# Attention and FFN block in float32: interleaved projections, or projections first by seven block products

## The chip, the core and the metric

The kernel runs on one core of a Trainium2 chip. The core has a matrix engine (TensorE, in the profile PE, its weight loads PEld), a vector engine (VectorE, DVE), a scalar engine (ScalarE, ACT), a general engine (GpSimd, POOL) and a queue engine (SyncE, SP). Each works off its own list of instructions in order and waits on semaphores for the others. SyncE, GpSimd and ScalarE can issue DMAs between DRAM and the on-chip memory SBUF. TensorE writes only to PSUM, eight banks of 128 partitions by 512 float32. The metric is the device time in microseconds, a median of three runs.

## The reference

The input x is 4 batches of 512 tokens by 1024, all float32.

```python
xn = _layernorm(x, axis=-1)
# attention: 32 query heads, 8 key/value heads, head size 128
qkv = xn @ w_qkv                      # 1024 -> 4096 + 1024 + 1024
scores = einsum('bqhgd,bkhd->bhgqk', q, k) * scale
bias = where(rel >= 0, -slopes * sqrt(rel), -inf)      # causal, per head
attn = softmax(scores + bias, axis=-1)
attn_out = einsum('bhgqk,bkhd->bqhgd', attn, v).reshape(B, S, 4096) @ w_o
# FFN: one 1024 x 1024 linear layer, and a routed low-rank part
ffn = xn @ W.T + b
probs = softmax(xn @ gate_w.T + gate_b)                # 4 ranks: 8, 16, 32, 64
ffn += weight * (xn @ A[:r].T @ B[:, :r].T)            # r of the top choice
return x + attn_out + ffn
```

## The kernel before

Float32 products are made from three passes. Every operand is split into a high part (float32r, written by ScalarE, `high`, L572) and a low part (the rest, subtracted by VectorE, `low`, L735), and `product` (L306 to L308) multiplies high by high, high by low and low by high into the same PSUM bank. A "product" of two tiles is thus three matmuls.

The work is cut into two pairs of batches (1024 tokens, eight tiles of 128). For each pair the tokens are loaded into `acc`, which is also the accumulator of the whole result. They are normalised by ScalarE (L645), transposed by TensorE (L360) and split into `x_hi` and `x_lo`, tile by tile (`before_groups`). Meanwhile TensorE already multiplies the tile before with the FFN weights. Then come the gate, the masks of the low-rank part, and the keys, values and first query of group 0. The transposed x stays in SBUF for the whole pair.

Then loops run over eight groups (one key/value head with four query heads), and in each over eight units (a query head and a batch). One unit is: causal scores of four row tiles (`scores`), maxima with the bias on VectorE (L766), exponentials on ScalarE (L605), a division by the row sum on VectorE (L777), ten transposes of 128 by 128 (L438), their split (L572, L735), and attention times values (`attend`). TensorE's list is software-pipelined: `one_group` puts the transposes of unit n-1 ahead of the scores of unit n, then the projection of the next unit's queries (24 matmuls of 512 columns), then attend of unit n-1, then a half of the next group's keys or values (12 matmuls). After four units each, `heads_burst` multiplies two heads' outputs with `w_o` for all 16 tiles of the result (96 matmuls) and VectorE adds them to `acc` (L810). Weights come as tiles of 128 by 1024 in two staging buffers, loaded by SyncE in the order of `group_loads` and split in the order of `SPLIT_IN`. GpSimd only stores the results (L294) at the end of each pair. The order is written by hand, and the loops are hardware loops.

## Time and profile before

| what | value |
|---|---|
| median of three runs | 2686.69 us (2684.19 to 2686.73) |
| span of the profiled execution | 2678.9 us |
| median less span | 7.8 us |
| TensorE busy | 2638.4 us, 98% |
| VectorE busy | 1581.6 us, 59% |
| ScalarE busy | 872.4 us, 33% |
| mean granted TensorE clock | 0.996 of full speed |
| DMA | 112.65 MB, mean 42 GB/s |

The span runs from the first to the last instruction; the profile gives no time of its own for what lies around it, so the median stands in for it. Matmuls overlap in the records, so the pace of TensorE is read from the starts and not from the busy time of one. Where a line is that of a helper (`high`, `low`, `product`), the names of the tiles tell what is done.

### The profile page before, as it was taken

Reading aid. Unit: us, or ns where it says so; the run is one execution under the profiler, and the core shown is the slowest. Engines: PE = TensorE matmul, PEld = TensorE weight load, DVE = VectorE, ACT = ScalarE, POOL = GpSimd, SP = SyncE. Lnnn points to the kernel's source line nnn. Section 1 sums busy time; section 2 is a strip of 40 time slices with the busy share of each in tenths; the row PEclk is TensorE's granted clock in tenths of the full one; section 3 lists DMA queues with packets and bytes.
Section 4 is the critical chain, followed back from the end, with each engine's and each line's share of the span. In section 5 each row is a group of like instructions: output and inputs, shape, how many; then the busy total and the mean of one; then the engine's idle time right before and its main releaser. Section 6 shows DMA issues by size and latency. Waiting matters only on the chain.

```text
span 2678.9 us, 37766 instructions
## 1 busy us (share of the span) xinstructions
PE 2638.4 (98%) x13280; PEld 2241.8 (84%) x13280; DVE 1581.6 (59%) x3492; ACT 872.4 (33%) x1966; POOL 10.5 (0%) x23
## 2 busy tenths in 40 slices
PE   7999999999999999999989999999999999999998
PEld 6788888888888888888767888888888888888887
DVE  6545556556556556566565455565565556556565
ACT  3133323333333333333231333333343323333332
POOL 0000000000000000000000000000000000000000
PEclk9999999999999999999989999999999999999999
DMA  3111011101010101101221101011010110011011
GB/s 120 51 48 32 24 39 32 47 32 39 31 39 31 38 24 32 47 31 40 87 92 52 48 32 40 23 37 42 31 45 25 40 40 32 26 37 39 32 40 63
DMA packets 31053, 112.65 MB, mean 42 GB/s; under 512 B 3498, under 2 KB 3642, under 8 KB 30972
## 3 DMA queue, kind: packets, MB, share of 16 engines
q1 hardware_dynamic: 26220, 94.49, 10.7%
q10 hardware_dynamic: 2304, 8.39, 0.9%
q0 software_dynamic: 2448, 8.67, 0.8%
q8 instruction: 53, 0.87, 0.1%
q14 instruction: 28, 0.23, 0.0%
HBM read 103.15 MB, written 8.39 MB: 42 GB/s over the span
## 4 chain that ended last, share of the span: by engine, by line
PE 97%; DVE 1%; issue 1%; ACT 0%; DMA 0%; ACTq 0%; POOL 0%; DVEq 0%; POOLq 0%
PE ps_q L306 11%; PE ps_q L308 11%; PE ps_q L307 11%; PE ps_kv L308 7%; PE ps_kv L307 7%; PE ps_kv L306 7%; PE ps_t L438 4%; PE ps_c L306 4%; PE ps_c L308 4%; PE ps_c L307 4%; PE ps_b L307 4%; PE ps_b L308 3%; PE ps_b L306 3%; PE ps_o L306 3%; PE ps_o L307 3%; PE ps_o L308 3%
## 5 line engine op out<-in xcount | busy, mean ns | idle before, releaser
L306 PE MATMUL ps_q<-x_hi,wq_hi 128*128 128x512 f32 x1024 | 399.6, 390 | 0.0
L308 PE MATMUL ps_q<-x_hi,wq_lo 128*128 128x512 f32 x1024 | 399.3, 390 | 0.0
L307 PE MATMUL ps_q<-x_lo,wq_hi 128*128 128x512 f32 x1024 | 398.6, 389 | 0.0
L605 ACT ACTIVATE probs<-probs,neg_max 128x512 f32<-128x512 f32 (+3 forms) x512 | 281.8, 552 | 344.2 <-DVE neg_max L766 344.2
L572 ACT ACTIVATE pt_hi<-ps_t 128x512 fp32r<-128x512 f32 x256 | 139.2, 596 | 641.4 <-PE ps_t L438 641.4
L735 DVE TENSOR_TENSOR pt_lo<-ps_t,pt_hi 128x512 fp32r<-128x512 f32 x256 | 164.8, 685 | 171.2 <-ACT pt_hi L572 171.2
L308 PEld LDWEIGHTS ps_q<-x_hi,wq_lo 128*128 128x128 f32 x1024 | 192.2, 188 | 41.4
L307 PEld LDWEIGHTS ps_q<-x_lo,wq_hi 128*128 128x128 f32 x1024 | 192.3, 188 | 36.0
L306 PEld LDWEIGHTS ps_q<-x_hi,wq_hi 128*128 128x128 f32 x1024 | 192.2, 188 | 35.5
L308 PE MATMUL ps_kv<-x_hi,wkv_lo 128*128 128x512 f32 x448 | 175.9, 393 | 0.0
L307 PE MATMUL ps_kv<-x_lo,wkv_hi 128*128 128x512 f32 x448 | 175.1, 391 | 0.0
L306 PE MATMUL ps_kv<-x_hi,wkv_hi 128*128 128x512 f32 x448 | 174.6, 390 | 0.0
L735 DVE TENSOR_TENSOR at_lo<-ps_o,at_hi 128x512 fp32r<-128x512 f32 x128 | 88.5, 691 | 144.6 <-ACT at_hi L572 144.6
L777 DVE TENSOR_SCALAR probs<-probs,row_inv 128x128 f32<-128x128 f32 (+3 forms) x512 | 163.3, 383 | 4.5
L306 PE MATMUL ps_o<-pt_hi,v_hi 128*128 128x512 f32 (+3 forms) x512 | 164.7, 322 | 0.0
L307 PE MATMUL ps_o<-pt_lo,v_hi 128*128 128x512 f32 (+3 forms) x512 | 164.6, 322 | 0.0
L308 PE MATMUL ps_o<-pt_hi,v_lo 128*128 128x512 f32 (+3 forms) x512 | 164.1, 320 | 0.0
L810 DVE TENSOR_TENSOR acc<-ps_kv,acc 128x512 f32<-128x512 f32 x152 | 105.0, 691 | 95.9 <-PE ps_kv L308 94.6
L572 ACT ACTIVATE at_hi<-ps_o 128x512 fp32r<-128x512 f32 x128 | 76.6, 598 | 258.1 <-PE ps_o L308 258.1
L572 ACT ACTIVATE q_hi<-ps_q 128x512 fp32r<-128x512 f32 x128 | 76.6, 598 | 251.8 <-PE ps_q L308 251.8
L810 DVE TENSOR_TENSOR acc<-ps_q,acc 128x512 f32<-128x512 f32 x152 | 105.0, 691 | 88.9 <-PE ps_q L308 88.8
L810 DVE TENSOR_TENSOR acc<-ps_c,acc 128x512 f32<-128x512 f32 x144 | 99.4, 690 | 80.7 <-PE ps_c L308 79.6
(267 smaller groups left out, 5589.5 us busy)
## 6 DMA issues: line engine op xcount, KB each, us to landing
stage<-w_qkv SPq DMA_DIRECT2D x98, 512.0 KB, 3.3
stage<-w_o SPq DMA_DIRECT2D x64, 512.0 KB, 3.2
acc<-x ACTq DMA_DIRECT2D x16, 512.0 KB, 4.2
stage<-w_ffn SPq DMA_DIRECT2D x16, 512.0 KB, 3.3
out<-acc POOLq DMA_DIRECT2D x16, 512.0 KB, 2.9
stage<-w_ag SPq DMA_DIRECT2D x2, 272.0 KB, 4.1
stage<-w_lora SPq DMA_DIRECT2D x2, 260.0 KB
dist<-consts POOLq DMA_DIRECT2D x1, 256.0 KB, 3.8
```

The costliest lines, as they stand in the source:

```text
L306: pe.matmul(to, st_hi, mv_hi, start=start, stop=False)
L307: pe.matmul(to, st_hi, mv_lo, start=False, stop=False)
L308: return pe.matmul(to, st_lo, mv_hi, start=False, stop=stop)
L438: last = pe.transpose(to[:, c * P:(c + 1) * P], probs[:, OFF[i] + j * P:OFF[i] + (j + 1) * P], ident[:, :])
L572: nc.scalar.activation(to, source, ACT.Copy).then_inc(signal, 1)
L605: nc.scalar.activation(tile, tile, ACT.Exp, bias=neg_max[:, i:i + 1], scale=-1.0, accum_out=row_sum[:, i:i + 1]).then_inc(s_exp, 1)
L735: nc.vector.tensor_tensor(to, source, high.bitcast(F32), ALU.subtract).then_inc(signal, 1)
L777: last = nc.vector.tensor_scalar(tile, tile, row_inv[:, i:i + 1], None, ALU.mult)
L810: nc.vector.tensor_tensor(to, banks[r % len(banks)][:, :], to, ALU.add).then_inc(s_acc, 1)
```

## The change

Almost every line is new. The program has two phases, written out without loops.

**Projections.** x is no longer multiplied with 128-column weight tiles of a group, but with whole 1024 by 1024 matrices: values, keys, four of queries (eight heads each), and the FFN. Per pair of batches each is a product of a 1024 by 1024 block of tokens with a 1024 by 1024 matrix. Both sides are cut in two by two blocks of 512. Strassen's scheme (in Winograd's form) needs seven block products (`STEPS`) instead of eight; each step has 16 products of 128 by 512 (48 matmuls) in four banks, and two sets of four banks take turns. Three steps begin a fresh sum in their banks, the other four add to what a step before left there. The seven operands of x (four sums of blocks among them) are made once per pair, in `operands`, by VectorE and ScalarE, and stay in SBUF. The block sums of the weights are made in place for each matrix in `weight_sums`. After each step the four banks leave PSUM in `leave`, by ScalarE after steps 0, 2 and 3, by VectorE after 1, 4 and 5, by both after 6, into two SBUF buffers `res_a` and `res_b`. Four finished blocks per matrix are split into high and low and stored to DRAM by GpSimd, 1 MB per part: queries and keys in pieces of 2 KB, values in pieces of 512 bytes (four DMAs per part). The FFN's blocks are added to x and stored as the accumulator's start. The gate's matmuls and transposes stand in the middle of some steps (`between`), the low-rank part in steps 1, 5 and 6 of the FFN.

**Attention.** 128 units again. Their queries, keys and values are loaded from DRAM, already split. TensorE's list per unit is scores of n, transposes of n-1, two tiles of the output projection (`fill_in`, 24 matmuls) of the set of four heads before, attend of n-1. The accumulator is loaded from DRAM before, stored after each pair.

```diff
-            def one_group(pr, g, last_group):
-                for n in range(UNITS):
-                    if n:
-                        transposes(pr, g, n - 1, last_group)
-                    scores(pr, g, n)
...
-                        next_queries(pr, g, n, last_group)
-                    if n:
-                        attend(pr, g, n - 1)
-                    if n == 4:
-                        heads_burst(pr, g, 0, range(0, BTILES // 2), last_group)
...
+MATRICES = 7
+VALUES, KEYS, Q0, FFN, Q1, Q2, Q3 = range(MATRICES)
+QUERIES = {Q0: 0, Q1: 1, Q2: 2, Q3: 3}
+STEPS = 7
+STARTS = (0, 1, 3)
+OPERANDS = (0, 1, 5, 3, 2, 4, 6)
...
+            def step(pr, m, st):
+                n = number(pr, m, st)
+                extra = {1: (0, 0), 5: (0, 1), 6: (1, 0)}.get(st) if m == FFN else None
+                for kt in range(KT):
+                    if kt % 2 == 0:
+                        weights_ready(n, kt // 2)
+                    if kt == 2:
+                        between(pr, m, st)
+                    for s in range(4):
+                        if kt == 0:
+                            free(n, s)
+                            if m == VALUES:
+                                pe.wait_ge(s_x_lo, 7 * (4 * pr + s) + OPERANDS.index(st) + 1)
+                                if st == 1:
+                                    pe.wait_ge(s_t_raw, 4 * 4 * (pr + 1))
+                            if m == FFN + 1 and st == 0:
+                                pe.wait_ge(s_lora_in, 4 * pr + s + 1)
+                            if m == FFN and st == 1 and s == 0:
+                                pe.wait_ge(s_u_lo, 2 * (pr + 1))
+                                pe.wait_ge(s_lora_lo, pr + 1)
+                        last = product(bank_of(n, s)[:, :], *operand(n, kt, s),
+                                       kt == 0 and st in STARTS,
+                                       kt == KT - 1 and extra is None)
+                        if kt == KT - 1 and extra is not None:
+                            last = lora(bank_of(n, s), s, *extra, False)
+                        if kt == 1 and s == 3:
+                            last.then_inc(s_first, 1)
+                        if kt == KT - 1:
+                            last.then_inc(s_bank, 1)
...
+            def fill_in(s, tt, half, f):
+                pr, g, b, _ = unit(s * G)
+                if f % 8 == 0:
+                    pe.wait_ge(s_at_lo, G * (s + 1))
+                    pe.wait_ge(s_wo_lo, G * (s // 2 + 1))
+                if f >= 2:
+                    pe.wait_ge(s_acc, f - 1)
+                t, cols = tt % QT, slice(half * 512, (half + 1) * 512)
+                for h in range(G):
+                    last = product(fill[f % 2][:, :],
+                                   (at_hi[:, s % 2, h, t * P:(t + 1) * P], at_lo[:, s % 2, h, t * P:(t + 1) * P]),
+                                   (wo_hi[:, g % 2, h, cols], wo_lo[:, g % 2, h, cols]), h == 0, h == G - 1)
+                last.then_inc(s_fill, 1)
...
+            for n in (TOTAL - 2, TOTAL - 1):
+                for s in range(4):
+                    pe.wait_ge(*drained(n, s))
+            for n in range(UNITS + G + 1):
+                if n < UNITS:
+                    scores(n)
+                if 1 <= n <= UNITS:
+                    transposes(n - 1)
+                for f in fills(n):
+                    fill_in(*f)
+                if 1 <= n <= UNITS:
+                    attend(n - 1)
...
+        @block.scalar
...
+            def leave(n):
+                pr, m, st = place(n)
+                if m == FFN:
+                    return
+                if st in (0, 2, 3):
+                    res = res_b if st == 2 else res_a
+                    if st == 2:
+                        act.wait_ge(s_store_b, stores_r(pr, m, 0))
+                    else:
+                        act.wait_ge(s_store_a, stores_r(pr, m, 0 if st == 0 else 1))
+                    for s in range(4):
+                        act.wait_ge(s_bank, 4 * n + s + 1)
+                        high(res[:, s, :], bank_of(n, s)[:, :], s_drain_a)
+                    return
+                i = {1: 0, 4: 1, 5: 2, 6: 3}[st]
+                if st == 6:
...
+                high(res_hi[:, :, :], (res_b if st == 5 else res_a)[:, :, :], s_res_hi)
...
+        @block.vector
...
+            def operands(pr):
+                deviation(pr, 0)
+                reciprocals(pr, 0)
+                if pr == 0:
+                    weights(0, 0)
+                    weights(0, 1)
+                for t in range(QT):
+                    i = pr * QT + t
+                    ps = [bank_of(number(pr, VALUES, 1), c)[:, :].rearrange("p (k c) -> p k c", k=KT) for c in range(4)]
+                    mine = slice(t * P, (t + 1) * P)
+                    for c, (slot, source) in enumerate(((0, 0), (1, 1), (5, 3))):
+                        dve.wait_ge(s_x_hi, 7 * i + c + 1)
+                        low(x_lo[:, slot, :, mine], ps[source], x_hi[:, slot, :, mine], s_x_lo)
+                    dve.wait_ge(s_b12, i + 1)
+                    nc.vector.tensor_tensor(t_raw[:, 1], t_raw[:, 0], ps[0], ALU.subtract).then_inc(s_t_raw, 1)
+                    dve.wait_ge(s_t_raw, 4 * i + 1)
+                    nc.vector.tensor_tensor(t_raw[:, 2], ps[3], t_raw[:, 1], ALU.subtract).then_inc(s_t_raw, 1)
+                    nc.vector.tensor_tensor(t_raw[:, 0], ps[3], t_raw[:, 0], ALU.subtract).then_inc(s_t_raw, 1)
+                    dve.wait_ge(s_t_raw, 4 * i + 3)
+                    nc.vector.tensor_tensor(t_raw[:, 3], ps[1], t_raw[:, 2], ALU.subtract).then_inc(s_t_raw, 1)
+                    if t + 1 < QT:
+                        deviation(pr, t + 1)
+                    for c, (slot, source) in enumerate(((3, 1), (2, 2), (4, 0), (6, 3))):
+                        dve.wait_ge(s_x_hi, 7 * i + c + 4)
+                        low(x_lo[:, slot, :, mine], t_raw[:, source], x_hi[:, slot, :, mine], s_x_lo)
+                    if t + 1 < QT:
+                        reciprocals(pr, t + 1)
+            def weight_sums(pr, m, st):
+                a11, a12, a21, a22 = (r[:, :] for r in raw)
+                g = pr * MATRICES + m
+                if st == 0:
+                    dve.wait_ge(s_raw[2], 16 * (g + 1))
+                    dve.wait_ge(s_raw[3], 16 * (2 * g + 1))
+                    nc.vector.tensor_tensor(a22, a21, a22, ALU.add).then_inc(s_sum, 1)
+                    dve.wait_ge(s_sum, sums(pr, m) + 1)
+                    nc.vector.tensor_tensor(a21, a11, a21, ALU.subtract).then_inc(s_sum, 1)
+                    dve.wait_ge(s_w_lo, split(number(pr, m, 0), 1))
+                    dve.wait_ge(s_sum, sums(pr, m) + 2)
+                    nc.vector.tensor_tensor(a11, a22, a11, ALU.subtract).then_inc(s_sum, 1)
+                if st == 1:
+                    dve.wait_ge(s_w_lo, split(number(pr, m, 1), 1))
+                    dve.wait_ge(s_sum, sums(pr, m) + 3)
+                    nc.vector.tensor_tensor(a12, a12, a11, ALU.subtract).then_inc(s_sum, 1)
...
+                if st in (1, 4, 5):
+                    res = res_b if st == 5 else res_a
+                    for s in range(4):
+                        dve.wait_ge(*drained({1: n - 1, 4: n - 1, 5: n - 3}[st], s))
+                        add(res, n, s)
+                if st == 6:
+                    dve.wait_ge(s_store_b, stores_r(pr, m, 1))
+                    for s in range(4):
+                        dve.wait_ge(s_last_hi, 4 * plain(pr, m) + s + 1)
+                        low(res_b[:, s, :], bank_of(n, s)[:, :], res_hi[:, s, :], s_drain_v)
+            def results(n):
+                pr, m, st = place(n)
+                if m == FFN or st not in (1, 4, 5):
+                    return
+                res = res_b if st == 5 else res_a
+                dve.wait_ge(s_res_hi, 3 * plain(pr, m) + {1: 0, 4: 1, 5: 2}[st] + 1)
+                low(res[:, :, :], res[:, :, :], res_hi[:, :, :], s_res_lo)
...
+            for pr in range(PAIRS):
+                operands(pr)
+                for m in range(MATRICES):
+                    for st in range(STEPS):
+                        n = number(pr, m, st)
+                        weights(n + 1, 0)
+                        if m or st:
+                            leave(n - 1)
+                        if st == 1:
+                            weight_sums(pr, m, st)
+                        if m or st:
+                            results(n - 1)
+                        weights(n + 1, 1)
+                        if st == 0:
+                            weight_sums(pr, m, st)
+                        gate_parts(pr, m, st)
...
+            for n in range(UNITS + G + 1):
+                if 2 <= n < UNITS + 2:
+                    outputs(n - 2)
+                if n < UNITS:
+                    maxima(n)
+                if 1 <= n <= UNITS:
+                    transposed(n - 1)
+                todo = fills(n)
+                for f in todo[:1]:
+                    add_fill(*f)
+                if n < UNITS:
+                    normalise(n)
+                    if n and chunk_in(n) is not None:
+                        out_weights(chunk_in(n))
+                for f in todo[1:]:
+                    add_fill(*f)
...
+        @block.gpsimd
...
+                    for c, (i, j, res, signal) in enumerate(((0, 0, res_a, s_store_a), (1, 1, res_a, s_store_a),
+                                                             (0, 1, res_b, s_store_b))):
+                        pool.wait_ge(s_res_hi, lo + c + 1)
+                        store(m, pr, i, j, 0, res_hi[:, :, :].bitcast(F32), s_store_h)
+                        pool.wait_ge(s_res_lo, lo + c + 1)
+                        store(m, pr, i, j, 1, res[:, :, :], signal)
+                    pool.wait_ge(s_last_hi, 4 * (plain(pr, m) + 1))
+                    store(m, pr, 1, 0, 0, res_hi[:, :, :].bitcast(F32), s_store_h)
+                    pool.wait_ge(s_drain_v, drained(number(pr, m, 6), 3)[1])
+                    store(m, pr, 1, 0, 1, res_b[:, :, :], s_store_b)
...
```

The order of the built programs shows it at three places. First TensorE in the middle of the attention units; `k_hi,q_hi` or `k,q` are scores, `ident,probs` transposes. Before:

```order
L438 MATMUL ps_t<-ident,probs 128x128 [waits s_probs]
L438 MATMUL ps_t<-ident,probs 128x128 x7
L438 MATMUL ps_o<-ident,probs 128x128 [waits s_at_lo]
L438 MATMUL ps_o<-ident,probs 128x128
L447 REGISTER_ALU
L306 MATMUL ps_c<-k_hi,q_hi 128x512 [waits s_q_lo]
L307 MATMUL ps_c<-k_lo,q_hi 128x512
L308 MATMUL ps_c<-k_hi,q_lo 128x512
```

and now, from the last scores of a unit on (`wo_hi,at_hi` is the output projection, twelve rows of which follow one another twice):

```order
L444 MATMUL ps<-k,q 128x256
L606 MATMUL ps<-ident,probs 128x128 [waits s_probs]
L606 MATMUL ps<-ident,probs 128x128 x7
L606 MATMUL ps<-ident,probs 128x128 [waits s_at_lo]
L606 MATMUL ps<-ident,probs 128x128
L442 MATMUL ps<-wo_hi,at_hi 128x512 [waits s_wo_lo,s_at_lo]
L443 MATMUL ps<-wo_lo,at_hi 128x512
L444 MATMUL ps<-wo_hi,at_lo 128x512
```

Transposes have moved behind the scores of the next unit, and what stands between them and attend are products of the head outputs with `w_o` instead of projections of x.

Second VectorE where x is prepared, for one tile before (`acc<-ps` adds an FFN product):

```order
L833 SCALAR_TENSOR_TENSOR next_k<-next_k 128x1 [waits s_link]
L916 REGISTER_ALU
L735 TENSOR_TENSOR x_lo<-ps_b,x_hi 128x4x128 [waits s_x_hi]
L916 REGISTER_ALU
L735 TENSOR_TENSOR x_lo<-ps_c,x_hi 128x4x128 [waits s_x_hi]
L807 ISA
L810 TENSOR_TENSOR acc<-ps_q,acc 128x512 [waits s_burst]
L807 REGISTER_ALU
L810 TENSOR_TENSOR acc<-ps_kv,acc 128x512 [waits s_burst]
L818 BN_STATS next_k<-acc 128x6 [waits s_x3]
L818 BN_STATS next_k<-acc 128x6
```

and for a pair of tiles now (`x_lo` splits an operand, `t_raw` are block sums):

```order
L832 TENSOR_TENSOR x_lo<-ps,x_hi 128x4x128 [waits s_x_hi] x3
L883 TENSOR_TENSOR t_raw<-t_raw,ps 128x512 [waits s_b12]
L885 TENSOR_TENSOR t_raw<-ps,t_raw 128x512 [waits s_t_raw]
L886 TENSOR_TENSOR t_raw<-ps,t_raw 128x512
L888 TENSOR_TENSOR t_raw<-ps,t_raw 128x512 [waits s_t_raw]
L848 BN_STATS stats<-rows 128x6 [waits s_rows0]
L848 BN_STATS stats<-rows 128x6
L848 BN_STATS stats<-rows 128x6 [waits s_rows1]
L848 BN_STATS stats<-rows 128x6
L851 BN_AGGR moments<-stats 128x2 [waits s_link]
L851 BN_AGGR moments<-stats 128x2
L854 TENSOR_SCALAR root<-moments 128x2 [waits s_link]
```

The adds of FFN products are gone from between the tiles; statistics of the next tiles stand between two halves of the splits of these.

Third GpSimd. Before, its first work after the constants is at the end of a pair:

```order
L294 ISA [waits s_acc]
L294 DMA out<-acc 128x1024
L293 REGISTER_ALU
L294 ISA [waits s_acc]
L294 DMA out<-acc 128x1024
L297 ISA
```

and now, for the keys of the first pair, eight stores of 1 MB in the order of the results:

```order
L374 DMA qk_s<-res_hi 128x4x512 [waits s_res_hi]
L374 DMA qk_s<-res_a 128x4x512 [waits s_res_lo]
L374 DMA qk_s<-res_hi 128x4x512 [waits s_res_hi]
L374 DMA qk_s<-res_a 128x4x512 [waits s_res_lo]
L374 DMA qk_s<-res_hi 128x4x512 [waits s_res_hi]
L374 DMA qk_s<-res_b 128x4x512 [waits s_res_lo]
L374 DMA qk_s<-res_hi 128x4x512 [waits s_last_hi]
L374 DMA qk_s<-res_b 128x4x512 [waits s_drain_v]
```

Each store waits for its own part, and later stores stand behind it in the same queue.

## Rows read from the trace of the kernel before

**Rows 1.** The page's first part: span, then each engine's busy time, share, instructions.

```profile
span 2678.9 us, 37766 instructions
PE 2638.4 (98%) x13280; PEld 2241.8 (84%) x13280; DVE 1581.6 (59%) x3492; ACT 872.4 (33%) x1966; POOL 10.5 (0%) x23
```

**Rows 2.** The page's chain that ended last, shares by engine.

```profile
PE 97%; DVE 1%; issue 1%; ACT 0%; DMA 0%; ACTq 0%; POOL 0%; DVEq 0%; POOLq 0%
```

**Rows 3.** Timeline (start, us, engine, line, op): twelve matmuls between these starts.

```profile
704.66 0.39 PE L306 MATMUL ps_q<-x_hi,wq_hi 128*128 128x512 f32 x1
...
707.38 0.39 PE L306 MATMUL ps_q<-x_hi,wq_hi 128*128 128x512 f32 x1
```

**Rows 4.** Timeline, TensorE: one unit with 24 projection matmuls.

```profile
1221.86 0.50 PE L306 MATMUL ps_c<-k_hi,q_hi 128*128 128x512 f32 x1 [0.32 <-DVE q_lo L735]
...
1223.88 0.40 PE L306 MATMUL ps_q<-x_hi,wq_hi 128*128 128x512 f32 x1
...
1229.34 0.39 PE L306 MATMUL ps_o<-pt_hi,v_hi 128*128 128x512 f32 x1
...
1231.24 1.03 PE L438 MATMUL ps_t<-ident,probs 128*128 128x128 f32 x8
...
1232.25 0.48 PE L306 MATMUL ps_c<-k_hi,q_hi 128*128 128x512 f32 x1
```

**Rows 5.** Timeline: the start of the program.

```profile
4.66 2.54 DVE L818 BATCH_NORM_STATS2 next_k<-acc 128x6 f32<-128x512 f32 x4 [4.66 <-DMA acc<-x]
...
8.99 0.16 DVE L833 SCALAR_TENSOR_TENSOR next_k<-next_k 128x2 f32<-128x2 f32 x1
...
9.19 1.24 ACT L645 ACTIVATE probs<-acc,next_k 128x1024 f32<-128x1024 f32 x1 [1.01 <-DVE next_k L833]
...
10.48 1.97 PE L360 MATMUL ps_t<-ident,probs 128*128 128x128 f32 x8 [10.48 <-ACT probs L645]
...
14.63 1.28 DVE L735 TENSOR_TENSOR x_lo<-ps_t,x_hi 128x512 fp32r<-128x512 f32 x2
```

**Rows 6.** Windows: us, then PE, PEld, DVE, ACT, POOL busy, PEclk, DMA share, GB/s.

```profile
0.00:10.00 10.00, 0.00 (x0) 0.00 (x0) 3.90 (x12) 2.30 (x3) 1.95 (x7) 1.00 0.68 243
...
1340.00:1350.00 10.00, 3.54 (x16) 3.14 (x16) 5.60 (x14) 5.15 (x7) 0.00 (x0) 0.60 0.48 168
```

**Rows 7.** Groups by line and form: busy us, mean ns, idle before.

```profile
L810 DVE TENSOR_TENSOR acc<-ps_kv,acc 128x512 f32<-128x512 f32 x152 | 105.0, 691 | 95.9 <-PE ps_kv L308 94.6
...
L735 DVE TENSOR_TENSOR wo_lo<-stage,wo_hi 128x1024 fp32r<-128x1024 f32 x76 | 92.5, 1220 | 5.0 <-ACT wo_hi L572 5.0
...
L572 ACT ACTIVATE wo_hi<-stage 128x1024 fp32r<-128x1024 f32 x76 | 79.2, 1047 | 35.7 <-PE ps_o L308 20.7 <-PE ps_c L308 9.9 <-DMA stage<-w_ffn 5.2
```

**Rows 8.** Timeline: an issue of POOL beside an add of VectorE.

```profile
1336.16 0.53 POOL L294 DMA_DIRECT2D out<-acc  x1 [1.42 <-DVE acc L810]
1336.17 0.69 DVE L810 TENSOR_TENSOR acc<-ps_q,acc 128x512 f32<-128x512 f32 x1 [0.67 <-PE ps_q L308]
```

**Rows 9.** The page's DMA queues: packets, MB, share of 16 engines' span.

```profile
q1 hardware_dynamic: 26220, 94.49, 10.7%
```

**Rows 10.** Timeline, VectorE: the unit of rows 4.

```profile
1223.25 0.68 DVE L766 CUSTOM_DVE_ANT_0 probs<-ps_c,head_bias 128x512 f32<-128x512 f32 x1
...
1226.30 0.18 DVE L773 RECIPROCAL row_inv<-row_sum 128x4 f32<-128x4 f32 x1 [1.33 <-ACT probs L605]
...
1226.51 1.27 DVE L777 TENSOR_SCALAR probs<-probs,row_inv 128x128 f32<-128x128 f32 x4
...
1232.07 0.69 DVE L735 TENSOR_TENSOR at_lo<-ps_o,at_hi 128x512 fp32r<-128x512 f32 x1 [1.02 <-ACT at_hi L572]
...
1232.68 1.28 DVE L735 TENSOR_TENSOR pt_lo<-ps_t,pt_hi 128x512 fp32r<-128x512 f32 x2
```

**Rows 11.** Timeline: the end of the program.

```profile
2672.11 0.39 PE L308 MATMUL ps_kv<-wo_hi,at_lo 128*128 128x512 f32 x1
...
2673.88 0.53 POOL L294 DMA_DIRECT2D out<-acc  x1 [2.19 <-DVE acc L810]
```

1366 lines of the change are left out of this document (697 added, 669 removed).

## The prediction

> **What bounds the kernel now.** I read the page's totals and the chain of waits first, then the timeline around single units, then the groups by line and the DMA part. The totals and the chain say that TensorE is the bound: it is busy 98% of 2678.9 us and holds 97% of the chain [rows 1, 2]. So time is the number of matmuls times their pace, plus the places where TensorE stands still. Busy time overlaps between matmuls, so the pace comes from starts. Twelve 512-column matmuls start between 704.66 and 707.38: 0.2267 us each [rows 3]. An attention unit that has 24 such matmuls beside its own work runs from 1221.86 to 1232.25, 10.39 us, and its neighbours take 10.37 and 10.38; minus 24 x 0.2267 = 5.44 this leaves 4.94 us for scores (2.0), ten transposes (1.0) and attend (1.9) [rows 4]. That one unit is the model of every unit of the changed kernel, since there, too, 24 matmuls stand between scores and attend.
>
> As a check of this reading on the kernel itself: it has 8640 matmuls of 512 columns (FFN 864, keys, values and queries 4608, output projection 3072, gate 96), so 8640 x 0.2267 = 1959 us; 128 units x 4.94 = 632; 256 transposes of x and of the values, some 28. Sum 2619. The other 60 us of the span are start, middle and end. The median of the runs is 7.8 us above the span; I add that at the end.
>
> **What the change removes.** In place of eight block products per matrix and pair of batches there are seven, so 4704 matmuls instead of 5376 for the seven matrices: 672 x 0.2267 = 152 us less. The LoRA and gate matmuls stay 96 and 96, the output projection 3072; the 128 transposes of the values go (values come out of the matmul already the right way round), 14 us at 0.11. TensorE's bare work is then 7968 x 0.2267 = 1806, + 632 + 13 (128 transposes of x) + 3 = 2454 us.
>
> **What it adds where TensorE waits.** I follow the queues of each engine in program order.
>
> Preparation of x, twice. Before, VectorE prepares a tile while TensorE multiplies the one before. Now a batch pair must be normalised, transposed and split into seven operands with VectorE in between, and step 1 cannot start until VectorE is through all of it. Per tile pair VectorE does 7 splits and 4 sums of 512 columns (0.61 apart, 0.69 each with a wait before it: 7.2 us with three waits), four statistics (2.54), the small chain (about 2), and waits some 4.4 us for ScalarE's two scalings and the transposes, which go at 1.97 us per eight at the start, where TensorE has been idle [rows 5]; ScalarE's scaling of the second tile ends 2.4 us after the first begins. That is 16.2 us per tile pair, 64.8 for four, less 4.2 that the last has not (statistics and small chain of a next one), plus 1.4 for the weights of step 1 behind them: 62. Pair 0 also waits for ScalarE, which now has the first weights ahead of the square root: the 1 MB behind 1.5 MB of x lands near 10 us at 243 GB/s [rows 6], so the first scaling starts near 14.9 instead of 9.2 [rows 5]. Step 1 starts near 77 us, with 17 us of useful work behind it: 60 us lost. Pair 1: 6 us to the scalings, 62 behind it: 51 us lost. If TensorE's clock stayed up, the transposes would halve and each tile pair would save up to 1.7 us, 14 in all; the row for it is the middle of the kernel, where the granted clock is 0.60 in the stretch in which TensorE is busy 3.54 of 10 us [rows 6], so near its lower level of 1.2 GHz, and I take the slow transposes.
>
> Projection steps. 48 matmuls, 10.88 us. Per matrix VectorE has 14 weight splits of 1024 columns (1.22 [rows 7]), four sums of twice that (2.3), 12 adds and 4 splits of 512 (0.69 [rows 7]), three splits of 2048 (2.3): 44 us of 76. ScalarE has 14 x 1.05 [rows 7], 16 x 0.6 and 3 x 2: 30 us. The tightest chain is sums, then the weights of step 2: VectorE ends the third sum 15.1 us after step 0 starts, the split of step 2's first weights ends at 17.4, needed at 21.8. That is 4.4 us of slack, so these are at nothing, if a step's results leave in time. The loads are 5 MB and the stores 8 MB in 76 us, 171 GB/s, where 0.68 of the DMA engines moved 243 [rows 6].
>
> Stores. One buffer holds the high parts, and the low parts of the last two results share another. The high part of step 5 goes out 3.5 us before a matrix ends, its low part 1.1 us before. VectorE must have the second landed by 8.3 us into the next matrix, or it holds the bank of step 1 and the sums. Fixed part: 0.54 to issue [rows 8], some 1.5 to land. A packet of about 3.6 KB costs 0.107 x 16 x 2678.9 / 26220 = 0.175 us of one engine [rows 9]. With 2 KB rows, 1 MB is 32 per engine: 3.1 us if time goes with bytes, 5.6 if it goes with packets. Two of them land at 4.8 to 9.8 us: no stall, or 1.5 us for each of the ten key and query matrices, 15 in all. I take 0, nearer to the bytes. Values go out in 512-byte rows, 128 per engine for 1 MB: 3.1 us by bytes, 22.4 by packets; the eight stores of a matrix then take 25 or 179 us beside its 76, so 0 to 105 us per pair. No row shows short pieces; I take about 8 us per store, which stalls the end of that matrix by 10, 20 for both.
>
> The Trainium skill, DMA: Bandwidth & Descriptors, section Specifications, has line rate from 512 bytes per piece on. By that the 20 would be 0 and the sum 2622; no run so far shows it.
>
> FFN end: its last result needs x from DRAM in a buffer whose store must land first: store and load, 5.3 + 5.0 + 0.1 + 5.5 = 16 us into step 6, then five adds to 20, while TensorE is through at 16.3 (24 LoRA matmuls, 5.4, lengthen that step): 4 us, 8 for both.
>
> Into attention. VectorE waits for the distance table, which POOL may load only behind the last two stores: near 10 us after the last matmul. Then four bias tiles (1.9), and four output-weight splits with two loads between, 8.2: the first maxima come at 20 where 1 would be ideal: 19 us. The first four units have no output tiles in them, and the loop scores, maxima, exponentials, normalise, transposes, split, attend takes 7.2 instead of 4.94: with the first one's latency 11 us, and 5 for the low clock.
>
> Units. VectorE per unit: maxima 1.7, three splits 1.7, at_lo 0.69, normalise 1.5, two adds 1.38, and in every other four units bias 0.48 and weights 1.22: 7.0 or 8.7 of 10.38 us [rows 7, 10]. Placed on TensorE's clock from the start of scores, at_lo ends at 1.5 (needed by the third transposed bank at 2.8), the probabilities are split at 5.3 (needed at 8.6), and the second add ends at 10.1, before the next at_lo at 11.2. So TensorE keeps 10.38. End: 6.8 us from the last matmul, as now [rows 11].
>
> **Sum.** 2454 + 60 + 51 + 20 + 8 + 19 + 16 + 7 = 2635 us of span; + 7.8 = 2642 us, 1.7% less than 2686.7. The saved 166 us are mostly spent on waits.
>
> **Rivals.** *Waits hidden better (2608 us, chance 0.22).* Value stores go with bytes and the clock holds: 20 + 14 less. For: 0.68 of the engines move 243 GB/s in 4 KB rows. Against: the granted clock of 0.60 in the one gap like it.
>
> *Stores set the end of each matrix (about 2725 us, chance 0.23).* The slower side. Place: the wait for the low buffer at the start of the next matrix. If a 512-byte piece costs 0.12 us (midway), the values' stores take 120 us beside 76, some 50 per pair: 100; keys and queries 15: 2642 - 20 + 115 = 2737, a little less where they overlap the first wait. It decides from 45 us of such stalls on. Against: 4 KB rows are fast. For: all stores now go through one POOL queue, in order.
>
> The Trainium skill, SBUF — State Buffer, section SBUF: two separate sides, speaks against the change: while VectorE runs certain operations that take both its ports, GpSimd cannot write the descriptors of its DMAs. Here the row is a POOL issue of 0.53 us beside an add of VectorE that starts with it [rows 8], so no block; but that add reads PSUM, and the sums of the changed kernel read SBUF twice. By the rule each of two issues per matrix could wait one sum of 2.3 us: 14 x 4.6 = 64 more, 2706.
>
> *VectorE bounds the units (about 2700, 0.05).* If its 8.7 us became 11.3, 64 units would each lose 0.9: 58. Against: the count above, with 1.7 us free.
>
> *Gain and waits cancel (0.06).* 37 to 50 us more of waits than counted.
>
> The order of the built program has 4704 projection matmuls, so that it doesn't do what it says is not a case.
>
> **How the numbers follow.** Forecast 2642 with 0.44, own range 2620 to 2675. Faster: 0.44 + 0.22 = 0.66; within 0.2% (about what a measurement tells from no change) 0.06; slower 0.23 + 0.05 = 0.28. Range 2598 to 2730: both rivals are inside, the extreme price of short pieces is left out.
>
> **What would show it.** Right: steps of 10.9 us in the projections, units of 10.38, TensorE's first projection step after step 0 near 77 us, a gap near 20 us before attention. Wrong: steps past 11.5 us with TensorE waiting for a drained bank, VectorE waiting for a POOL store, units above 10.5, or an "issue" share above the 1% of now [rows 2].

## The result and the profile after

The changed kernel takes 2695.33 us (median of 6 runs, 2692.59 to 2695.93), the kernel before 2686.36 (6 runs, 2684.19 to 2686.73): a ratio of 1.0036, 95% interval 1.0025 to 1.0048. It is slower by 9 us. The prediction said 2642 and faster. The profiled execution took 2695.61 us and has a span of 2693.8 us.

The first lines of the page answer to [rows 1, 2]: span; busy time, share and instructions of each engine; and the chain that ended last.

```profile
span 2693.8 us, 32243 instructions
PE 2504.9 (93%) x12480; PEld 2135.8 (79%) x12480; DVE 1654.5 (61%) x3352; ACT 1026.9 (38%) x2127; POOL 140.1 (5%) x201
PE 86%; DVE 7%; DMA 3%; ACT 2%; issue 1%; POOL 0%; SPq 0%; DVEq 0%; ACTq 0%; POOLq 0%
```

The work did shrink: 800 instructions fewer on TensorE, 134 us less of busy time. But TensorE's idle time rose from 40 to 189 us, and the chain is on TensorE for 86% instead of 97%. The question is where TensorE stands still.

First the places where it does not. TensorE's timeline (start, us, engine, line, operation) has the same matmul of two successive projection steps, and the first scores of two successive units, which answer to [rows 3, 4]:

```profile
182.96 0.39 PE L443 MATMUL ps<-x_lo,w_hi 128*128 128x512 f32 x1
...
193.84 0.39 PE L443 MATMUL ps<-x_lo,w_hi 128*128 128x512 f32 x1
...
1405.39 0.39 PE L442 MATMUL ps<-k,q 128*128 128x512 f32 x1
...
1415.79 0.39 PE L442 MATMUL ps<-k,q 128*128 128x512 f32 x1
```

A step takes 10.88 us and a unit 10.40, as forecast (10.9, 10.38). By windows (us, busy time of PE, PEld, DVE, ACT, POOL, then PEclk, DMA share, GB/s) of one undisturbed stretch of attention and of the two preparations, which answer to [rows 6]:

```profile
80.00:264.00 184.00, 184.00 (x819) 149.66 (x818) 104.61 (x113) 66.87 (x80) 30.75 (x42) 1.00 0.48 157
...
1400.00:2600.00 1200.00, 1200.00 (x6690) 1057.58 (x6689) 853.93 (x2306) 530.45 (x1441) 8.49 (x16) 1.00 0.31 108
0.00:80.00 80.00, 32.35 (x124) 27.45 (x125) 51.34 (x98) 36.29 (x50) 1.46 (x6) 0.81 0.31 110
658.00:729.00 71.00, 28.81 (x116) 24.30 (x116) 46.46 (x99) 35.06 (x51) 1.50 (x2) 0.71 0.28 101
```

From 80 to 264 us, with all the values' and keys' stores in it, TensorE is never idle. The preparations cost what was forecast: step 1 starts at 74.74 (77 forecast), and 70.4 us after the last matmul of pair 0 (68). Three other kinds of gap are left. **The LoRA gap.** TensorE's timeline around step 1 of the FFN matrix in the first pair of batches; what ended the idle time stands in brackets:

```profile
324.17 0.39 PE L444 MATMUL ps<-w_hi,x_lo 128*128 128x512 f32 x1
343.21 0.77 PE L442 MATMUL ps<-w_hi,x_hi 128*128 128x512 f32 x1 [18.65 <-DVE lora_lo L832]
343.77 0.63 PE L443 MATMUL ps<-w_lo,x_hi 128*128 128x512 f32 x1
...
346.76 0.59 PE L444 MATMUL ps<-w_hi,x_lo 128*128 128x512 f32 x1
347.19 0.39 PE L442 MATMUL ps<-w_hi,x_hi 128*128 128x512 f32 x1
347.42 0.40 PE L443 MATMUL ps<-w_lo,x_hi 128*128 128x512 f32 x1
```

It waits 18.8 us for the low part of the LoRA operand (19.04 between the two starts, less the 0.23 of one matmul), and 18.4 us for the same at 976.7. Behind the gap the matmuls start 0.43 apart until 347, then 0.23: at the lower clock level these nine matmuls take 1.9 us more. Whose work is late shows on the other engines, here GpSimd, ScalarE and VectorE of the same stretch:

```profile
317.21 0.75 POOL L374 DMA_DIRECT2D qk_s<-res_hi  x1 [3.97 <-ACT res_hi L659]
321.23 0.75 POOL L374 DMA_DIRECT2D qk_s<-res_b  x1 [3.27 <-issue]
321.97 0.76 POOL L386 DMA_DIRECT2D res_a<-x  x1
326.87 0.56 POOL L388 DMA_DIRECT2D lora_raw<-w_lora  x1 [4.14 <-DMA qk_s<-res_b]
331.75 1.06 ACT L659 ACTIVATE lora_hi<-lora_raw 65x1024 fp32r<-65x1024 f32 x1 [14.84 <-DMA lora_raw<-w_lora]
332.71 1.04 ACT L659 ACTIVATE w_hi<-raw 128x1024 fp32r<-128x1024 f32 x1
333.78 1.22 DVE L832 TENSOR_TENSOR w_lo<-raw,w_hi 128x1024 fp32r<-128x1024 f32 x1 [13.61 <-ACT w_hi L659]
334.93 2.28 DVE L904 TENSOR_TENSOR raw<-raw,raw 128x2048 f32<-128x2048 f32 x1
...
339.64 2.29 DVE L909 TENSOR_TENSOR raw<-raw,raw 128x2048 f32<-128x2048 f32 x1
341.85 1.22 DVE L832 TENSOR_TENSOR lora_lo<-lora_raw,lora_hi 65x1024 fp32r<-65x1024 f32 x1
```

The operand goes into res_b, so its load waits for the last store of the third matrix to land. ScalarE sits on that load with the next weights queued behind it, and VectorE, which sits behind those weights, does a split and three sums before the one subtraction that TensorE needs. **Two small ones** on VectorE, in both pairs: the two one-row memsets ahead of u_lo, and the four LoRA additions (L935) behind a weight split and four other additions:

```profile
264.92 0.91 DVE L987 MEMSET u_hi<- 1x1024 f32 x1 [0.27 <-issue]
266.00 0.91 DVE L988 MEMSET u_lo<- 1x1024 f32 x1 [0.16 <-issue]
266.92 1.28 DVE L832 TENSOR_TENSOR u_lo<-ps,u_hi 64x512 fp32r<-64x512 f32 x2
...
423.28 1.23 DVE L832 TENSOR_TENSOR w_lo<-raw,w_hi 128x1024 fp32r<-128x1024 f32 x1 [9.91 <-ACT w_hi L659]
424.42 2.48 DVE L917 TENSOR_TENSOR res_b<-ps,res_b 128x512 f32<-128x512 f32 x4
426.81 2.47 DVE L935 TENSOR_TENSOR res_a<-ps,res_a 128x512 f32<-128x512 f32 x4
```

TensorE waits 3.7 us for the first (264.4 to 268.3) and 5.7 for the second (421.8 to 427.6). **The entry into attention**, last projection matmul, first scores, next scores, and two rows of ScalarE and VectorE:

```profile
1310.26 0.39 PE L444 MATMUL ps<-x_hi,w_lo 128*128 128x512 f32 x1
1319.09 0.76 PE L442 MATMUL ps<-k,q 128*128 128x512 f32 x1 [8.45 <-DVE res_b L832]
1341.81 0.77 PE L442 MATMUL ps<-k,q 128*128 128x512 f32 x1 [18.86 <-DVE neg_max L1045]
...
1324.91 1.90 DVE L1034 TENSOR_SCALAR bias<-dist,slopes 128x512 f32<-128x512 f32 x4 [6.18 <-DMA dist<-consts]
...
1336.17 1.06 ACT L659 ACTIVATE wo_hi<-wo_raw 128x1024 fp32r<-128x1024 f32 x1 [18.46 <-DMA wo_raw<-w_o]
```

The two gaps are 27.7 us (8.6 and 19.1); 19 were forecast. The distances allow VectorE to go on only at 1324.91, 14.4 us after the last projection matmul (forecast 10), and from there to its first maxima at 1340.97 it needs 16.1 us for bias tiles and weight splits (forecast 10.1), since the third row of the output weights arrives late. The theory taken to the experiments: a few instructions late in an engine's order, none of them heavy, cost TensorE 37 + 7 + 11 us outside the preparations and 28 at the entry, and each costs its gap plus about 2 us at the lower clock level. The rivals: the stores set it (the slower side of the prediction), or the waits share slack and come back elsewhere when one is removed.

### The profile page after: what moved, and what is told of

It reads as the page before. It is cut to its first block, busy times and chain, and to the rows that moved or that the text cites. A ratio compares the mean times of both kernels' runs of the same rounds, so it can differ in the third digit from the quotient of the medians.

```text
span 2693.8 us, 32243 instructions
## 1 busy us (share of the span) xinstructions
PE 2504.9 (93%) x12480; PEld 2135.8 (79%) x12480; DVE 1654.5 (61%) x3352; ACT 1026.9 (38%) x2127; POOL 140.1 (5%) x201
## 4 chain that ended last, share of the span: by engine, by line
PE 86%; DVE 7%; DMA 3%; ACT 2%; issue 1%; POOL 0%; SPq 0%; DVEq 0%; ACTq 0%; POOLq 0%
PE ps L442 27%; PE ps L444 27%; PE ps L443 27%; PE ps L606 5%; DMA qk_s<-res_b 1%; PE ps L518 1%; DVE x_lo L832 1%; DVE res_b L832 1%; DVE stats L848 1%; ACT w_hi L659 1%; DVE res_b L917 1%; ACT res_hi L659 1%; DVE w_lo L832 0%; ACT rows L693 0%; DMA raw<-w_all 0%
## 5 line engine op out<-in xcount | busy, mean ns | idle before, releaser
L832 DVE TENSOR_TENSOR w_lo<-raw,w_hi 128x1024 fp32r<-128x1024 f32 x196 | 239.4, 1224 | 441.9 <-ACT w_hi L659 441.8
L442 PE MATMUL ps<-x_hi,w_hi 128*128 128x512 f32 x1120 | 440.2, 393 | 18.0 <-DVE res_a L935 11.0
L443 PE MATMUL ps<-x_lo,w_hi 128*128 128x512 f32 x1120 | 439.2, 392 | 0.0
L444 PE MATMUL ps<-x_hi,w_lo 128*128 128x512 f32 x1120 | 438.9, 392 | 0.0
L442 PE MATMUL ps<-wo_hi,at_hi 128*128 128x512 f32 x1024 | 412.2, 403 | 1.4 <-DVE at_lo L832 1.4
L444 PE MATMUL ps<-wo_hi,at_lo 128*128 128x512 f32 x1024 | 401.0, 392 | 0.0
L443 PE MATMUL ps<-wo_lo,at_hi 128*128 128x512 f32 x1024 | 399.4, 390 | 0.0
L442 PEld LDWEIGHTS ps<-x_hi,w_hi 128*128 128x128 f32 x1120 | 212.2, 189 | 63.9 <-issue 11.8
L443 PEld LDWEIGHTS ps<-x_lo,w_hi 128*128 128x128 f32 x1120 | 212.2, 190 | 43.9
L832 DVE TENSOR_TENSOR pt_lo<-ps,pt_hi 128x512 fp32r<-128x512 f32 (+1 forms) x384 | 207.1, 595 | 22.3 <-ACT pt_hi L659 22.3
L1045 DVE CUSTOM_DVE_ANT_0 probs<-ps,bias 128x512 f32<-128x512 f32 (+3 forms) x512 | 219.5, 484 | 0.2
```

Of the source, the lines that this page charges most:

```text
L442: pe.matmul(to, st_hi, mv_hi, start=start, stop=False, skip_group_check=True)
L443: pe.matmul(to, st_hi, mv_lo, start=False, stop=False, skip_group_check=True)
L444: return pe.matmul(to, st_lo, mv_hi, start=False, stop=stop, skip_group_check=True)
L832: nc.vector.tensor_tensor(to, source, high.bitcast(F32), ALU.subtract).then_inc(signal, 1)
L1045: nc.vector.tensor_tensor_reduce(out=probs[:, n % 2, OFF[i]:OFF[i] + (i + 1) * P], in0=score_bank[i], in1=bias[:, h, SEQ - (i + 1) * P:SEQ ...
```

## The experiments

All are edits of the changed kernel. The kernel before, timed beside them on the same chips, took 2685.1 us (e1, e2, e3, e8), 2685.6 (e4 to e7) and 2684.6 (the kernels with all edits); ratios are to it, and their intervals are 2.4 to 4 us to either side. A gain in us is against the 2695.33 of the changed kernel, which was timed only beside the kernel before at 2686.36, so a chip's difference of 1 to 2 us is in it. In the diffs only the core is shown.

**Order alone (e1).** VectorE:

```diff
+ if m == FFN and st == 0: gate_parts(pr, m, st)      # lora_lo
  weights(n + 1, 1)
  if st == 0: weight_sums(pr, m, st)
- gate_parts(pr, m, st)
+ if m != FFN or st: gate_parts(pr, m, st)
```

> VectorE splits the LoRA operand (lora_lo) ahead of the second weight split and the three weight sums of the step, not behind them; the load of the operand stays where it is. Order theory (the wait of 18.8 and 18.4 us for lora_lo is a load that comes late, 331.75, and then three weight sums of 2.29 us and a split ahead of it in VectorE's order): the first matmul with lora_lo starts near 335, not 343.2, so about 8 us go per pair of batches, 16 in all: time about 2679. Rival, the weight sums pushed back are the next thing late: step 1's matrix then waits for its split instead, the gap only changes its name, and the time stays within 3 us of 2695. Rival, the load alone sets it: gap stays above 16 us, 2695.

Measured 2678.31 us, ratio 0.9979 (0.9970 to 0.9988). The gap is 9.6 us (322.73 to 332.59) and 9.7; no new wait behind it.

**Load alone (e2).**

```diff
- lora_raw = at("lora_raw", 176 * K, ...)             # res_b
+ lora_raw = at("lora_raw", 168 * K, ...)             # res_a
@@ GpSimd, third matrix, ahead of its last two stores
+ pool.wait_ge(s_store_a, stores_r(pr, FFN, 0))
+ pool.dma_start(lora_raw[0:LK, :], w_lora)...
@@ GpSimd, FFN
- pool.wait_ge(s_store_a, ...); load x -> res_a; pool.wait_ge(s_store_b, ...); load w_lora -> lora_raw
+ pool.wait_ge(s_lora_lo, pr + 1); load x -> res_a; pool.wait_ge(s_store_b, ...)
@@ ScalarE, ahead of lora_hi
+ act.wait_ge(*drained(number(pr, m, st) - 1, 3))
```

> The LoRA operand is loaded into res_a, which is free since step 4, ahead of the last two stores of the third matrix, not into res_b behind them; the load of x for the first block then waits for lora_lo. VectorE's order stays. Order theory: ScalarE's split no longer waits for a load and starts near 322.5, so w_hi, w_lo and the three sums all move forward 8 to 9 us and with them lora_lo, to about 333; the gap falls from 18.8 to about 10: 2695 - 2 x 8.5 = about 2678. Rival, the load of x now starts later (behind lora_lo) and is late for the first addition of the block: a new wait of some 5 us per pair before step 2, 2688. Rival, stores set it: nothing moves, 2695.

Measured 2679.18 us, ratio 0.9978 (0.9969 to 0.9987). The gap is 9.8 and 9.6 us; lora_hi starts at 322.52. The later load of x makes no wait.

**Both (e3).**

> Both edits of the LoRA operand together: loaded early into res_a, split ahead of the weight sums. Order theory: lora_lo is done near 325 to 326 and TensorE, which comes to it at 324.2, waits 1 to 2 us, not 18.8; with the matmuls at half clock after the gap (about 2 us each time) also gone, 2 x (17 + 2) = 38 us less: about 2657, by itself faster than the kernel before (2686). Rival, given back later: the weight sums and the load of x come late and half of it returns as waits in steps 1 to 3, about 2676. Rival, stores set the end of each matrix: within 5 us of 2695.

Measured 2656.14 us, ratio 0.9896 (0.9881 to 0.9912): 39.2 us less than the changed kernel, and 1% faster than the kernel before. ScalarE, VectorE and TensorE now:

```profile
322.55 1.06 ACT L660 ACTIVATE lora_hi<-lora_raw 65x1024 fp32r<-65x1024 f32 x1 [5.83 <-DMA qk_s<-res_hi]
323.65 1.22 DVE L834 TENSOR_TENSOR lora_lo<-lora_raw,lora_hi 65x1024 fp32r<-65x1024 f32 x1 [2.91 <-ACT lora_hi L660]
325.01 0.47 PE L443 MATMUL ps<-w_hi,x_hi 128*128 128x512 f32 x1 [0.66 <-DVE lora_lo L834]
```

18.7 us of waiting became 0.7. The first two edits cut the gap to half each, since either the load or the sums alone still hold lora_lo back to 331.22 and 332.62; together they are worth 39 where the single gains are 17 and 16. The 6 us between are mostly the clock: behind the gaps of 9.6 to 9.8 us the matmuls at the lower level still cost 2.8 to 3.0 us each time, behind the 0.7 only 0.3.

**LoRA additions one turn earlier (e4).** VectorE's four additions move from leave() of the next step's turn to the end of the turn of FFN step 6, with a wait for step 4's additions ahead.

> VectorE adds the four LoRA tiles of the last block in the loop's turn of the last step (FFN, step 6), right after its second weight split, not in the next step's turn behind a weight split and the four additions of step 6. Order theory: the 5.66 us gap at 421.8 and at 1073.8 goes, with the matmuls at half clock behind it (2.3 us each): 2 x 8 = 16 us less, 2679. Rival (the term of 4 us was put down to the load of x): the additions wait for a load that lands as late, and the gap stays above 4: 2695. Rival, given back: the weight split behind the additions is late instead and 5 of the 8 us return: 2689.

Measured 2680.73 us, ratio 0.9981 (0.9972 to 0.9990): 14.6 less. The additions start at 412.60, not behind those of step 6, and the gap is gone in both pairs. So the buffer reload to which the prediction gave this term was not what ended last.

**Memsets two steps earlier (e6).** nc.vector.memset of u_hi and u_lo moves from step 2 of the third matrix to step 0.

> The two one-row memsets of the LoRA input move from just ahead of its low parts to VectorE's work two steps earlier. Order theory: the 3.66 us gap falls by the two memsets (two times 1.1 us) to about 1.5, in both pairs, and the clock dips less: 5 us less, 2690. Rival (the memsets lie beside TensorE's transposes and ScalarE's copies, and the low parts wait for those): nothing, 2695.

Measured 2688.12 us, ratio 1.0009 (1.0000 to 1.0018): 7.2 less. VectorE, in place of the rows at 264.92 to 266.92:

```profile
263.01 1.22 DVE L832 TENSOR_TENSOR w_lo<-raw,w_hi 128x1024 fp32r<-128x1024 f32 x1
264.15 1.27 DVE L832 TENSOR_TENSOR u_lo<-ps,u_hi 64x512 fp32r<-64x512 f32 x2
```

The low parts start 1.1 us behind the start of the weight split, where they started 3.5 us behind it, and the gap falls from 3.7 to 1.3 us. That is 2.3 us per pair from the order; with the matmuls at the lower clock level behind the longer gap (1.7 and 1.5 us) it comes to 7.9, of which 7.2 are measured. I had counted the clock at next to nothing here.

**Entry (e5).**

```diff
@@ SyncE, ahead of attention's first loads (was: GpSimd, behind the last stores)
+ sp.dma_start(dist[:, :], consts[:, 0:SEQ]).then_inc(s_dist, 16)
@@ chunk_in(n): the first four rows of the output weights, one per unit
+ if n < G: return n
@@ ScalarE and VectorE, ahead of unit 0
- for c in range(G): out_weights(c)
```

> Entry into attention: the distances are loaded by SyncE ahead of the first queries, not by GpSimd behind the last stores, and the first four rows of the output weights are loaded and split one per unit in the first four units, not all ahead of the first unit. Order theory: scores of unit 1 start near 1320, not 1341.8, since the last stores land earlier too (fewer loads beside them); of the 21 us the four splits (1.2 us each on VectorE, which sets these first units) give 5 back: 2679. Rival, the loads of k, q and the last stores set it (8.6 of the 27.7 us are a wait for stores): the second gap turns into a wait for q, only 5 us gained: 2690.

Measured 2680.19 us, ratio 0.9979 (0.9970 to 0.9988): 15.1 less. The second gap is gone, but the first grew from 8.6 to 11.0: VectorE's last drain waits 12.8 us for a store of res_b that was issued at 1307.01, beside the loads of k, q, v and the output weights. ScalarE's last drain, which VectorE's needs, waits 10.4 us for the store of res_hi before it.

**Preparation (e7).** VectorE does reciprocals(pr, t + 1) ahead of the four low parts of tile t.

> In the preparation VectorE works out the next tile's scaling (five small operations, 1.0 us) ahead of the four low parts of this tile (2.5 us), not behind them. Order theory: a tile's turn of 15.0 us, bound by VectorE with 3.1 us of it idle behind ScalarE's scaling, becomes 12.5 to 13: six turns in all, 13 us less, 2682. Rival, VectorE then waits for ScalarE's square root (which stands behind four copies) and gains nothing: 2695. Rival, the time goes, but TensorE's clock, lower in longer idle stretches, is as low: changes nothing here, since the preparation is set by VectorE.

Measured 2684.99 us, ratio 0.9995 (0.9986 to 1.0004): 10.3 less. Tiles follow each other in 12.8 to 13.1 us instead of 15.0 (TensorE's transposes at 31.14, 43.90, 57.02), and step 1 starts at 68.28. The forecast of this run was 13.

**Smaller pieces for all stores (e8).** The test of the rival that the prediction feared most:

```diff
- pool.dma_start(qk_s[b, first:first + 4, :, level, :]..., source)
+ for t in range(4):
+     cut = slice(128 * t, 128 * (t + 1))
+     pool.dma_start(qk_s[b, first:first + 4, :, level, cut]..., source[:, :, cut])
```

> Every store of queries and keys is cut into four DMAs with pieces of 512 bytes, as those of the values are; the bytes are the same. Theory that stores have slack (the values' stores with such pieces made no wait): the time stays within 5 us of 2695; GpSimd's issues go from 1 to 4 per store at 0.75 us, and only the entry into attention, which waits for the last stores, and the wait for the LoRA operand behind a store grow, 3 us each: 2695 to 2705. Rival of the prediction (stores set the end of each matrix; the 20 us were right but small): steps 1, 5 and 6 wait for drained banks, VectorE's 27 us of waits for stores double and reach TensorE: 12 matrices by 3 to 5 us, 2730 to 2755.

Measured 2718.43 us, ratio 1.0130 (1.0115 to 1.0146): 23.1 us more than the changed kernel, between the two theories' figures, so neither number held. By DMA issues (count, KB each, median us to landing), changed kernel first:

```profile
qk_s<-res_hi POOLq DMA_DIRECT2D x40, 1024.0 KB, 4.7
qk_s<-res_a POOLq DMA_DIRECT2D x20, 1024.0 KB, 9.1
qk_s<-res_b POOLq DMA_DIRECT2D x20, 1024.0 KB, 5.2
v_s<-res_a POOLq DMA_DIRECT2D x16, 256.0 KB, 7.5
```

```profile
qk_s<-res_hi POOLq DMA_DIRECT2D x160, 256.0 KB, 3.7
qk_s<-res_a POOLq DMA_DIRECT2D x80, 256.0 KB, 7.6
qk_s<-res_b POOLq DMA_DIRECT2D x80, 256.0 KB, 4.4
```

VectorE's waits for these stores before its writes to res_b (us, times), changed kernel first:

```profile
  DMA qk_s<-res_b: 27.5, 10
```

```profile
  DMA qk_s<-res_b: 60.7, 10
```

So VectorE's waits doubled, as the rival said. Where TensorE's 23 us are says how much of this reached it. Read from TensorE's starts in both traces, its waits grow at the two LoRA gaps (18.8 to 22.7 and 18.4 to 22.3), before the second preparation (3.0) and at the entry (4.0), four places that wait for a last store, 15 us; another 5 come between the values and the third matrix of the second pair and 1 in the first pair. There VectorE, held for 5.2 and 4.3 us by a store at the end of the keys (0.8 before), is late with the gate, and TensorE's transposes in the third matrix wait for it, 2.7 and 1.9 us. That is the rival's mechanism at a small size. In the three matrices behind the FFN VectorE's waits for stores also grew, from 1.4 to 2.1 us each to 4.8 to 6.6, but TensorE waits for nothing there: they took 230.7 us and take 231.4 (230.6 and 230.9 in the second pair).

The edit changes two things at once, the length of the pieces and the number of issues. GpSimd's four issues of a store take 2.98 us where one takes 0.75, while a piece lands sooner after its own issue (4.4 us, not 5.2, for res_b). So the later end of a store lies mostly in the issues, and the price of short pieces by themselves is not shown: a store of 512-byte pieces in one DMA was not run.

**All five edits (e3 to e7) together.**

> The five edits together (LoRA operand loaded and split early; LoRA additions in the last step's turn; memsets early; entry with early distances and spread output weights; preparation with the scaling ahead of the low parts). Order theory, each wait stands alone on TensorE's way: the single gains add up, 39.2 + 14.6 + 7.2 + 15.1 + 10.3 = 86 us, time 2609. Rival, the gaps share slack (stores, weight loads and VectorE had time to catch up in them, and steps now run into each other): a fifth or more comes back as short waits, 2625 or above.

Measured 2606.21 us, ratio 0.9708 (0.9695 to 0.9721). The single gains sum to 86.5, together they are 89.1, the same within the intervals: nothing came back.

**And the first loads of attention earlier.** SyncE waits for step 2 of the last matrix instead of step 5 ahead of k, q, v; only the distances and output weights wait for step 4.

> As the one with all five, and the first loads of attention (k, q, v, the first rows of the output weights, the distances) go out two to three steps earlier, as soon as their places are free, not together with the last stores. Theory: the last two stores landed 10 to 12 us after their issue beside 3 MB of such loads (5 us elsewhere), and VectorE's last drain waited for one of them; without the loads beside them scores start 4 us after the last projection matmul, not 11: 7 us less than the one with all five, 2602. Rival, the stores are as slow by themselves (or held back by the weight loads): nothing, 2609. Rival, the early loads now stand beside the stores of the step before and move the wait there: nothing or worse, 2609 to 2613.

Measured 2597.88 us, ratio 0.9678 (0.9665 to 0.9692): 8.3 less. The gap before the first scores is 3.7 us, not 11.1: VectorE's last drain still waits for the store of res_b, but that now lands 4.9 us after its issue (1230.79 to 1235.74) and not 12.3 (1232.01 to 1244.33).

**And the second pair's first scaling ahead of the first pair's last drains.**

> As the one before, and the statistics and the scaling of the second pair's first two row tiles come ahead of the last drains of the first pair (the rows were loaded long before). Theory: the gap of 13.8 us from the last matmul of pair 0 to the first transposes of pair 1 shrinks to the time that the drains take, about 8, 5 to 6 us less: 2597. Rival, the square root's table load (1.3 us) and the scaling (2.4 us) on ScalarE delay its drains, which set the start: gain below 2 us, 2600.

Measured 2595.02 us, ratio 0.9663 (0.9650 to 0.9677): 2.9 less, about half of what was expected. TensorE's timeline at the start of the second pair, of the kernel with all edits but this one first, and with it:

```profile
633.69 2.61 PE L523 MATMUL ps<-ident,rows 128*128 128x128 f32 x11 [13.45 <-ACT rows L698]
```

```profile
629.15 3.65 PE L523 MATMUL ps<-ident,rows 128*128 128x128 f32 x16 [9.10 <-DVE res_b L843]
```

The transposes start 4.3 us sooner behind the last matmul of the first pair (9.5 us, not 13.8) and now wait for VectorE's drain; the tiles behind them follow 13.1 to 13.7 us apart, not 12.8 to 13.1, which takes 0.9 back. Its five times (2592.67 to 2595.66) lie all below those of the kernel without this edit (2597.55 to 2600.16), so the 2.9 are real though the two intervals overlap. This last is the fastest kernel of the study, 3.4% faster than the kernel before.

## Why the prediction was wrong

Its size and its sign were both wrong. The span came out 59 us above the sum of 2635, the time 53 above 2642. The step that failed is the list of TensorE's waits: the wait for the LoRA operand and the slow matmuls behind each gap were in no term. By the prediction's own steps:

- **The removed work** was right: steps of 10.88, units of 10.40, TensorE busy 134 us less, though it ran part of this at the lower clock level, where a busy microsecond does less.
- **Preparation**, 60 + 51: measured 58 and 53. Right. The slow transposes were the right choice: the granted clock was 0.81 and 0.71 in these windows.
- **Stores of values**, 20: measured 0 on TensorE. The bounds of 0 and 105 per pair held, the value taken did not. The values' stores of 256 KB in 512-byte pieces landed in 7.5 us at most by median; VectorE and ScalarE waited up to 4.7 us for one of them, and TensorE was busy without a break from 80 to 264 us. The Trainium skill, DMA: Bandwidth & Descriptors, section Specifications, has line rate from 512 bytes per piece on. The missing stall fits that, though these landing times measure no rate.
- **FFN end**, 8: measured 11.3, and its cause was misread. I followed the buffer to its store and load and took the additions of step 6 and of LoRA as one run; the waiting matmul needed only the second, which VectorE does behind the first. e4 shows it. The load itself came as forecast: it was issued at 415.47 and lands in 5.7 us by median, which is 421.2, and TensorE was through at 422.0.
- **The LoRA operand**, in no term: 37.2 us of waiting, the largest error. The text follows the weight sums as the tightest chain of VectorE, with "4.4 us of slack, so these are at nothing, if a step's results leave in time", and never asks what stands behind them. In FFN step 0 that is lora_lo. It also speaks of the low part's buffer and its store, and not of the LoRA load that waits for the same store. The condition in that sentence was the place to look. e1, e2 and e3 show both halves: load 16, order 17, both 39.
- **u_lo**, in no term: 7.3 us. The two one-row memsets are 4.7 of them (e6); the rest, 1.3 us per pair, stays.
- **Into attention**, 19: measured 27.7. The distances and splits were seen, but both were taken too short (14.4 us for 10, 16.1 for 10.1); the landing of the last stores in 10 us beside attention's first loads was not seen. The run with the early first loads shows that part: 8.3 us.
- **First units of attention**, 11 + 5: about right. From the first scores to those of unit 5 (1319.09 to 1374.20) it took 55.1 us; less the gap of 19.1 and the work of five scores and four rounds of transposes and attend at the 2.0, 1.0 and 1.9 us of the prediction, 14 are left.
- **Low clock behind the gaps**, in no term: 16.2 us. The 5 us of the sum stood for the first units of attention alone. Behind each of the gaps in the projections came 3.0 to 6.1 us of matmuls 0.43 us apart. Over eight places (step 1 behind each preparation, and the three gaps in each pair's projections) they cost 1.6 to 2.6 us each, read as the time by which the starts exceed 0.2267 each.
- **Median less span**, 7.8: measured 1.8. The profiled execution of the changed kernel took 2695.61 us with its span of 2693.8, and every execution of the kernel before that is listed with both has 1.9 to 2.1. The 7.8 set a median of 2686.69 against the span of a faster execution. This made the error of the time 6 us smaller than that of the span, which is luck.

For the span: + 37.2 (LoRA), + 7.3 (u_lo), + 3.3 (FFN end), + 8.7 (entry), + 16.2 (clock), + 2.5 (units, 123 times 0.02), + 1.2 (end, 8.0 for 6.8), and - 20 (values' stores) make 56 of the 59. The other 3 stay unassigned; the terms called right are off by up to 2 themselves.

**The rivals.** Stores did not hold TensorE at the ends of the matrices within a pair; what they do set is the LoRA operand, the start of the second pair and the entry into attention. Nor did VectorE bound the units. The one which came nearest is "gain and waits cancel", 37 to 50 us more of waits, to which I gave 0.06, though the kernel came out just beyond it (0.36% slower, where 0.2% was meant). It needed a mechanism and I had none in mind, so it got next to no chance. The block of GpSimd's issues would have given 2706, close to the time by accident. The rows speak against it: GpSimd's issue of a store stands inside a VectorE operation that reads SBUF twice, and takes 0.75 us like the others:

```profile
1303.59 2.29 DVE L832 TENSOR_TENSOR res_b<-res_b,res_hi 128x2048 f32<-128x2048 f32 x1 [2.06 <-ACT res_hi L659]
1303.85 0.75 POOL L374 DMA_DIRECT2D qk_s<-res_hi  x1 [4.79 <-ACT res_hi L659]
```

The Trainium skill, SBUF — State Buffer, section SBUF: two separate sides, has this block for VectorE's 2-port modes and, for operations with two SBUF inputs, only against a GpSimd operation that reads SBUF. The 64 us came from reading it for every such operation.

Of the promised signs for "right" three came, and the fourth in part: the gap near 20 at the entry was one of 19.1 behind one of 8.6. One for "wrong" came too: VectorE did wait for stores, 27.5 us in ten waits for queries and keys. The two longest are 10.4 us at the entry and 6.3 before the second preparation, where TensorE pays for them; the others are 0.8 to 2.1 us. None of the signs looked at the FFN matrix, so they could not have shown the error.

## What to carry to other kernels

When a change empties TensorE's schedule of spare work, go through every wait of TensorE, not the heaviest chain: for each one write down the instructions ahead of its producer in that engine's order, and what each of those waits for. A single 1.2 us subtraction behind three sums and a load behind a store cost 39 us, nearly all of the 45 that the change was forecast to gain. In this kernel the gains of such waits added up when they were removed together (86.5 and 89.1 us), provided both halves of a wait (the late load and the late place in the order) are taken as one edit.

## What the runs showed of the hardware that I had not expected

- A memset of one partition by 1024 elements takes 0.91 us on VectorE; a subtraction of 65 partitions by 1024 takes 1.22, one of 128 by 1024 also 1.22.
- GpSimd's issue of a rearranged store takes 0.75 us, for 1 MB in 2 KB rows and for 256 KB in 512-byte pieces alike; [rows 8] had 0.53 for a plain block.
- Stores of 1 MB from res_hi and res_b land in 4.7 and 5.2 us by median; the last ones took 10 to 12 beside 3 MB of loads, and the engine that reuses the buffer waited. Those from res_a land in 9.1 us by median, for which no run shows the reason; no engine is listed as waiting for one.
- The mean granted clock follows the gaps: 0.996 in the kernel before, 0.967 in the changed one, 0.984 with the five edits. Matmuls came back to 0.23 us apart 3 to 6 us after each gap, and the longer gap did not cost more: 2.8 to 3.0 us behind 9.6 to 9.8 us of waiting (e1, e2), 1.9 to 2.0 behind 18.4 to 18.8.
